# Up convolution of a fused convolution and attention kernel: eight weight matrices and a second, half-shifted image copy written by ScalarE

## The reference

```python
x = x + conv(_gn(x), bias, up_filter, dn_filter)      # depthwise part
t = to_tokens(x)                                      # (16, 1024, 32)
t = t + attention(_ln_t(t), Wq, Wk, Wv)               # causal, one head
t = t + ffn(_ln_t(t), gate_w, gate_b, weight1, weight2)  # 16 experts pick 8 tokens each
```

```python
x = x + bias
x = repeat(repeat(x, 2, axis=2), 2, axis=3)
x = conv_same(x, up_filter)             # 12 x 12 taps
x = leaky_relu(x, 0.2) * sqrt(2)
x = conv_same(x, dn_filter)[:, :, ::2, ::2]
```

## Time and profile before

| What | Value |
| --- | --- |
| Median of three runs | 368.54 us (368.35 to 369.02) |
| The profiled execution | 368.35 us, of which 366.5 us from its first to its last instruction |
| Mean granted TensorE clock | 0.948 |
| TensorE matmuls busy | 327.2 us (89%) x3362 |
| VectorE busy | 260.1 us (71%) x523 |
| ScalarE busy | 183.9 us (50%) x251 |
| GpSimd busy | 128.8 us (35%) x96 |
| `up` matmuls (L892 into psB) | 480, 56.4 us busy |
| The two DMAs that place parts of UU | issued at 18.7 us and behind, 0.60 and 0.73 us each to issue, 2.3 us to land |
| GpSimd's memsets at the start | the largest, 2560 f16 elements, 2.22 us; all done by 6.2 us, then idle to 17.0 us |

### The profile page before, as it was taken

One profiled execution on the slowest core, in us unless ns is written; L12 is line 12 of the kernel. 1 busy time (PEld: TensorE's weight loads), 2 busy tenths in 40 slices (PEclk: granted clock), 3 DMA queues, 4 the chain that ended last, 5 costly groups with the idle time before them and its releaser, 6 DMA issues.

```text
span 366.5 us, 8381 instructions
## 1 busy us (share of the span) xinstructions
PE 327.2 (89%) x3362; PEld 249.3 (68%) x3362; DVE 260.1 (71%) x523; ACT 183.9 (50%) x251; POOL 128.8 (35%) x96
## 2 busy tenths in 40 slices
PE   2289998799999999999899999999996986979985
PEld 1168886587777878786678787777774544546774
DVE  2679779957757877869686876776988786454632
ACT  1043355446557574757663755576564547440500
POOL 6134535332444337554211557312235400351000
PEclk9999999999999999999999999999999899995655
DMA  4910100001011010101000101011021100100122
GB/s 125 204 36 3 26 19 16 16 16 31 16 18 26 5 32 2 31 4 32 15 16 2 31 15 17 17 16 26 7 58 32 31 2 18 28 2 29 57 75 69
DMA packets 35906, 11.16 MB, mean 30 GB/s; under 512 B 24431, under 2 KB 35741, under 8 KB 35869
## 3 DMA queue, kind: packets, MB, share of 16 engines
q1 hardware_dynamic: 33152, 9.98, 11.3%
q10 hardware_dynamic: 2717, 0.66, 1.2%
HBM read 5.72 MB, written 4.21 MB: 27 GB/s over the span
## 4 chain that ended last, share of the span: by engine, by line
PE 77%; DVE 10%; DMA 5%; issue 3%; ACT 2%; POOL 1%; ACTq 1%; SPq 0%; DVEq 0%; POOLq 0%
PE psB L892 14%; PE psA L892 13%; PE psB L1025 9%; PE psB L1005 8%; PE psA L990 7%; PE psA L1070 4%; PE psA L882 3%; PE psA L1048 3%; PE psB L1039 3%; DVE negmax L757 2%; PE psA L993 2%; PE psA L983 2%; PE psA L1032 2%; PE psB L1008 2%; PE psB L977 2%
## 5 line engine op out<-in xcount | busy, mean ns | idle before, releaser
L757 DVE TENSOR_REDUCE negmax<-psA 128x1 f32<-128x512 f32 (+7 forms) x128 | 90.5, 751 | 32.2 <-PE psA L993 31.6
L587 ACT ACTIVATE Pp<-psB 128x1024 f32<-128x1024 f32 (+1 forms) x80 | 73.6, 937 | 35.3 <-PE psB L1008 30.7
L892 PE MATMUL psB<-xin,UU 128*128 128x224 f16 (+1 forms) x480 | 56.4, 277 | 0.1
L892 PE MATMUL psA<-y,DD 128*128 128x224 f16 (+1 forms) x480 | 55.1, 273 | 0.0
L990 PE MATMUL psA<-zK,yQ 128*128 128x512 f16 (+1 forms) x192 | 47.8, 332 | 6.0 <-DVE uT L775 2.4
L892 PEld LDWEIGHTS psB<-xin,UU 128*128 128x128 f16 x480 | 47.0, 99 | 7.9 <-DVE xin L698 0.5
L1005 PE MATMUL psB<-yQ,zK 128*128 128x512 f16 (+1 forms) x192 | 47.3, 330 | 3.7 <-DMA yQ<-rows 2.4
L892 PEld LDWEIGHTS psA<-y,DD 128*128 128x128 f16 x480 | 46.7, 98 | 5.5
L477 POOL TENSOR_TENSOR zrstd<-zrstd,power 128x8 f32<-128x8 f32 x16 | 27.2, 1698 | 53.9 <-DVE zrstd L735 53.9
L557 ACT ACTIVATE y<-psB 128x1024 f16<-128x1024 f32 x16 | 16.4, 1023 | 44.8 <-PE psB L892 44.8
L499 POOL TENSOR_TENSOR y<-y 128x1024 f16<-128x1024 f32 x16 | 34.1, 2132 | 9.8 <-ACT y L560 9.8
(11 more groups left out here) (158 smaller groups left out, 504.5 us busy)
## 6 DMA issues: line engine op xcount, KB each, us to landing
x_all<-in_x_dram SPq DMA_DIRECT2D x4, 512.0 KB, 3.9
normalised_tokens<-z SPq DMA_DIRECT2D x16, 128.0 KB, 1.8
zV<-normalised_tokens SPq DMA_DIRECT2D x64, 32.0 KB, 2.1
out_dram<-x_all SPq DMA_DIRECT2D x8, 256.0 KB, 2.3
yQ<-rows SPq DMA_DIRECT2D x32, 2.0 KB
Pp<-filter_tables ACTq DMA_DIRECT2D x4, 121.9 KB, 3.7
w_halves<-y SPq DMA_DIRECT2D x12, 32.0 KB, 1.8
cst<-shape_constants SPq DMA_DIRECT2D x1, 326.5 KB, 4.3
```

Source lines behind the costliest of these rows:

```text
L587: nc.scalar.activation(Pp[:, n % 2, UOFF[e[2]]:UOFF[e[2]] + N], slot(e)[:, 0:N], ACT.Exp).then_inc(b_drained, 1)
L757: ins = nc.vector.tensor_reduce(negmax[:, n % 2, m - 1:m], s[:, at:at + P * m], X, ALU.max, negate=True)
L892: ins = nc.tensor.matmul(within(out_cols, -shift), m, within(v, shift), start=i == 0, stop=i == len(matrices) - 1)
```

## The change

For images 2 to 15 the products with k = -1 and k = 1 of residues 1 and 2 are merged. Two more DMAs at the start copy the weights of k = -1 into the zero partitions of matrices 8 and 9 (`filter_wrap`), so that matrix 8 and matrix 9 each hold both sides. The image operand for them is a new tile `mixed`, a second copy of the image whose partitions 0 to 63 are moved by one column group to one side and whose partitions 64 to 127 are moved by one to the other. The columns that fall outside are zero: GpSimd clears the whole tile once, with one more memset behind its other ones. ScalarE writes `mixed` with two copies an image, each 64 partitions by 2 halves x 32 channels x 7 column groups = 448 elements, f16 to f16. The tile has two slots, for even and odd images. Residues 1 and 2 then have 6 matmuls each, all with 256 columns, and an image has 24 in place of 30. Images 0 and 1 keep the old way with 30; there the matmuls with k = 1 read partitions 0 to 63 alone.

A new event `mixed` for image t + 5 stands in step t behind `prob` unit 0 and ahead of `yQ`. ScalarE waits in it for the `up` of two images before and for the low halves of the image. TensorE waits in `up` for both copies.

```diff
+PLAIN_UP = 2
+def mixture(ahead):
+    return lambda t: ("mixed", t + ahead) if PLAIN_UP <= t + ahead < B else None
 STEP = [batch(1, "score", 2), once(-1, "image_low", 1), batch(3, "z_rstd"), once(3, "image_low", 2),
-        once(-8, "xT", 3), batch(0, "prob", 0), group(6, "logit_max"), batch(2, "yQ"), batch(-1, "pv"),
+        once(-8, "xT", 3), batch(0, "prob", 0), mixture(5), group(6, "logit_max"), batch(2, "yQ"), batch(-1, "pv"),
...
+        mixed = sb("mixed", [P, 2, 2, H, JW], F16)
...
+        def filter_wrap(r):
+            q, n = slice(C * r, C * r + C), r - 1
+            return (UU[q, :, SPAN - n:SPAN, :, :].rearrange("p i m q t -> p i (m q t)"),
+                    U_parts[q, :, 0:n, :, :].rearrange("p i m q t -> p i (m q t)"))
+        def mixture_halves(n):
+            at = BC * (n % GB)
+            v = xin[:, n // GB % 2, :].bitcast(F16).rearrange("p (i n) -> p i n", i=2)[:, :, at:at + BC].rearrange("p i (h j) -> p i h j", j=JW)
+            return [(mixed[rows, n % 2, :, :, to:to + JW - 1], v[rows, :, :, 1 - to:JW - to])
+                    for rows, to in ((slice(0, 2 * C), 0), (slice(2 * C, P), 1))]
...
+            for r in (R - 2, R - 1):
+                place_to, place_from = filter_wrap(r)
+                sp.dma_start(place_to, place_from).then_inc(UU_wrapped, 16)
...
+            nc.gpsimd.memset(mixed[:, :, :, :, :], 0.0).then_inc(mixed_zero, 1)
...
+                if name == "mixed":
+                    if n < PLAIN_UP + 2:
+                        act.wait_ge(mixed_zero, 1)
+                    else:
+                        act.wait_ge(b_filled, BU["up", n - 2] + 1)
+                    act.wait_ge(xin_ready, 2 * (n // GB) + min(n % GB, 1) + 1)
+                    for to, v in mixture_halves(n):
+                        nc.scalar.activation(to, v, ACT.Copy).then_inc(mixed_ready, 1)
...
+                        act.wait_ge(UU_wrapped, 16 * 2)
...
+                    if n >= PLAIN_UP:
+                        pe.wait_ge(UU_wrapped, 16 * 2)
+                        pe.wait_ge(mixed_ready, 2 * (n - PLAIN_UP) + 2)
+                    of = slice(BC * (n % GB), BC * (n % GB) + BC)
+                    parts = [v[:, of] for v in img[n // GB % 2]]
+                    both = [mixed[:, n % 2, j, :, :].rearrange("p h j -> p (h j)") for j in range(2)]
                     for t in range(R):
+                        if 1 <= t <= 2 and n >= PLAIN_UP:
+                            outer = [(UU[:, i, R - t + NS - 1, :, :], both[j], 0) for i, j in ((0, 0), (0, 1), (1, 0))]
+                        else:
+                            outer = [(UU[0:rows, i, R * k - t + NS - 1, :, :], parts[j][0:rows], k)
+                                     for k, rows in ((-1, P), (1, 2 * C if 1 <= t <= 2 else P)) if 0 <= R * k - t + NS - 1 < SPAN
+                                     for i, j in ((0, 0), (0, 1), (1, 0))]
                         ins = convolve(s[:, BC * t:BC * t + BC],
-                                       [(UU[:, i, R * k - t + NS - 1, :, :], parts[j], k) for k in (-1, 0, 1) if 0 <= R * k - t + NS - 1 < SPAN
-                                        for i, j in ((0, 0), (0, 1), (1, 0))])
+                                       [(UU[:, i, NS - 1 - t, :, :], parts[j], 0) for i, j in ((0, 0), (0, 1), (1, 0))] + outer)
```

More of the change, by code:

```diff
@@ L341, in hybrid_kernel @@
         U_ready = sem("U_ready")
-        UU_ready, UU_copied = sem("UU_ready"), sem("UU_copied")
+        UU_ready, UU_copied, UU_wrapped = sem("UU_ready"), sem("UU_copied"), sem("UU_wrapped")
+        mixed_zero, mixed_ready = sem("mixed_zero"), sem("mixed_ready")
         sums_ready, U_split = sem("sums_ready"), sem("U_split")
@@ L952, in _ @@
                         pe.wait_ge(UU_copied, 2)
-                    parts = [v[:, BC * (n % GB):BC * (n % GB) + BC] for v in img[n // GB % 2]]
-                    for t in range(R):
+                    if n >= PLAIN_UP:
[4 more added lines that the diff above has]
+                    both = [mixed[:, n % 2, j, :, :].rearrange("p h j -> p (h j)") for j in range(2)]
+                    for t in range(R):
+                        if 1 <= t <= 2 and n >= PLAIN_UP:
[4 more added lines that the diff above has]
+                                     for i, j in ((0, 0), (0, 1), (1, 0))]
                         ins = convolve(s[:, BC * t:BC * t + BC],
-                                       [(UU[:, i, R * k - t + NS - 1, :, :], parts[j], k) for k in (-1, 0, 1) if 0 <= R * k - t + NS - 1 < SPAN
-                                        for i, j in ((0, 0), (0, 1), (1, 0))])
+                                       [(UU[:, i, NS - 1 - t, :, :], parts[j], 0) for i, j in ((0, 0), (0, 1), (1, 0))] + outer)
                 elif name == "down":
```

## The result

The changed kernel took 370.73 us (369.76 to 370.96, 4 runs) against 368.45 us (367.96 to 369.02, 4 runs) before. The ratio is 1.0056, with a 95% interval of 1.0033 to 1.0080: slower by 0.3 to 0.8%. The forecast was 364.8 us, faster. Some executions run in a slower state of the chip, and the ratios leave these out while the medians do not, so a ratio need not be the quotient of two medians. So the change costs between nothing and 3 us; the 3.6 us forecast as gain are not there.

A forecast was written before the change was run, and what follows sets the result against it. TensorE, 89% busy, was taken to bound the kernel from 71 to 262 us. Opening +3.12, image 8 +0.5 and images 5 to 15 -7.22 make -3.6 us: 364.8 us, range 361.0 to 367.6.

The forecast's parts named there:

- A removed matmul is worth 109.4 ns, 0.656 us an image.: TensorE's up convolution: number of matmuls, not columns, sets the price; six fewer save 0.656 us an image, 0.48 by columns.
- A pair of copies is done after 1.06 us and holds ScalarE for 0.96.: ScalarE's two copies into `mixed`, 0.58 us each: they hold ScalarE for 0.96 us, with bounds of 0.64 and 1.1.
- the overlap of 0.1 us between neighbours: On ScalarE, a following instruction was taken to start about 0.1 us before the one ahead of it ends.
- the prediction's own formula: With p us for a pair on ScalarE, the opening loses 3 (p - 0.96) more and image 8 p - 0.96.
- The slower rival: ScalarE's copies in runs of 7 elements are dear: slower from p = 1.55 us, 374.8 us at p = 2.0; chance 0.08.
- The waits of images 2, 3 and 4, 3.12 us.: Opening: TensorE waits for the copies, net losses 1.48 and 1.01 us, and 0.63 at image 4 through VectorE's chain.
- The clock, a rival at 0.09.: TensorE's new idle time ahead of image 2 drops its clock, losing 1.6 us: 366.4 us; chance 0.09.
- "What costs nothing.": Start: the memset (0.9 us) fits GpSimd's idle time, the two DMAs are hidden, images 0 and 1 keep their matmul number.
- The middle costs nothing.: Images 9 to 15 and the like: oT and yQ come in time behind the copies, 0.5 us to spare; image 8 loses 0.5.

The follow-up runs named there:

- e3: Changed kernel without its copies, memset and wait, merged products reading the plain image (other output): 362.11 us, ratio 0.9811 to the kernel before.
- e5: Changed kernel plus filler matmuls in TensorE's idle time ahead of image 2 (nine) and image 3 (seven): 369.12 us, ratio 1.0021 to the kernel before.
- e6b: Changed kernel with 128-row matmuls for images 0 and 1, without the two weight DMAs and their waits: 369.14 us, ratio 1.0028 to the kernel before.
- e8: Changed kernel, old way for images 0 to 4, later memset, copies one image earlier except images 8 and 12: 365.62 us, ratio 0.992 to the kernel before.

## Why the prediction was wrong

By its own steps:

- **A removed matmul is worth 109.4 ns, 0.656 us an image.** Right: 0.661 in e3. The Trainium skill's gap formula ("TensorE: Matmul & The Clock Gate", Back-to-back issue gap), by columns, would have 0.50. These matmuls don't follow it; the section itself gives it for a single isolated matmul, and says that in a stream of weight loads and matmuls both set the spacing.
- **A pair of copies is done after 1.06 us and holds ScalarE for 0.96.** The copy was right, 0.576 us for 0.58; the pair was not. The step that failed is the overlap of 0.1 us between neighbours: a pair is done after 1.17 to 1.18 us and holds ScalarE for 1.20, above the upper bound of 1.1. By the prediction's own formula, 3 (p - 0.96) in the opening and p - 0.96 at image 8, that is an estimated 0.7 and 0.24 us. The slower rival (dear copies, p over 1.55 us) is not what happened.
- **The waits of images 2, 3 and 4, 3.12 us.** The mechanism was right, and the sizes were too small. Without the fall of the clock (e5, and e6b within 0.01) image 2 lost 1.66 us (1.48 forecast): 0.12 for the longer pair and 0.09 more from its end to the first matmul; in the changed kernel image 3 lost 1.35 (1.01) and image 4 0.54 by its end (0.63 for the chain).
- **The clock, a rival at 0.09.** It came true in the profiled execution. It was priced at 1.6 us and cost 1.7. I gave it too small a chance: my forecast itself made TensorE idle for 2 us ahead of image 2, and I had rows of a fall after an idle time at 282 that was 2.75 us long, but left it out of the sum.
- **"What costs nothing."** This step failed outright. The memset does lie in GpSimd's idle time, but I asked only what stands behind it on GpSimd, not whom it slows on VectorE: 0.9 us at the copy, 0.86 at the end of image 0 in this pair of traces. And the 64-row matmuls "are as many as before", but they cost 0.42 us in image 1.
- **The middle costs nothing.** I checked oT against `up` and yQ against the scores, and both held (e8 takes no more for it). I missed `proj` of steps 4 and 8, which stands ahead of the scores and needs oT: 0.40 + 0.39 us. At image 8 the loss was 0.97 for 0.5: 0.30 more from the low halves to the convolution, the pair above all, and 0.17 for its start after idle time. Images 6 and 12 lost 0.23 and 0.17, of which e8 gave back the first; their cause stays open.

The sum by dates: opening up to the end of image 5, +6.32, where the forecast had 3.12 - 0.66 = +2.46; of the 3.86 us between, 1.7 are the clock, 0.87 the memset, 0.42 the 64-row matmuls, and 0.9 are spread over images 2 to 5, of which the longer pair may be 0.7. Middle, -4.41 for -6.06: 0.79 `proj`, 0.47 more at image 8, 0.40 at images 6 and 12. The rest of the span after image 15 took 0.4 us less than before. That makes +1.5 us in the profiled execution. The median is 2.3 us above, with three of four runs at a mean clock of 0.940, below all runs of before whose clock is on record; which stretch of those runs lost the clock no trace here shows.

## What to carry to other kernels

Where a bound engine gets shorter, check the other engines' queues for every reader of what is pushed back, those of each fourth step too: here two things waited for oT, the banks of `up` and `proj`, and only the first was checked. Take the time that a pair of instructions holds an engine from a row of that pair, or give it a bound without overlap. In an opening that runs through several engines, work taken from the bound engine was worth little (e3, 0.85 of 2.6 us), and a wait put before it was paid in full, in idle time and in some traces again in clock; so begin such a change where the steady part begins, and put the new work where its engine already waits for the bound one. "In an idle time" is an answer for one engine only: ask who runs beside it at that time.

## What the runs showed of the hardware

- A VectorE copy of 12 f32 elements in SBUF that met GpSimd's memsets ended 0.02 to 0.04 us after the last of the row, in all twelve traces, whether it started at 5.46 or at 5.76 us. With one more memset of 1024 f16 elements (0.945 us) in the row it took 1.42 us in place of 0.43; so the 0.43 holds waiting too. The Trainium skill ("Advanced Engine Details and Errata", Miscellaneous Facts) says that GpSimd shares a read and a write interface with VectorE, and that this conflicts with VectorE instructions in a two-port mode or with two SBUF inputs. The rows agree with a conflict; they do not tell in which mode the copy ran, or which interface it was.
- At each switch between 64-row and 128-row weights the weight loads stood for 0.21 us, though half of the rows are unused. Four switches made 3.70 us of 30 matmuls in place of 3.28.
- ScalarE's copies of 64 x 448 f16 elements, in runs of 7, took 0.576 us and did not overlap with what came behind them: 1.17 to 1.18 us for two, and 0.02 to 0.03 us more to the next. Copies and exponentials of 128 x 1024 elements overlap by 0.1 us (1.02 us long, 0.92 to 0.93 apart).
- TensorE's clock fell after 2.1 us of idle time (image 2) and, when this was filled, at the next pause, ahead of image 3. With both filled (e5) it did not fall around these images. But e6b had both pauses and no fall, so the length of a pause alone does not decide it; what else does was not settled.
